# A decoder layer with four experts: the first tile of expert rows chosen from the first two batches, its choice spread over the last batch's scans

## The reference, cut to what matters

```python
x = layernorm(x + attention(x))          # 32 heads of 8, relative bias, softmax
x = layernorm(x + mamba(ctx_1024, z=x))  # conv, selective scan over 16 states, gated by silu(x)
# the experts, on all 1024 tokens:
probs = softmax(x @ Wr + br)             # 4 experts
top_w, top_idx = top_k(probs, 1)
y_e = (silu(x @ Wg[e]) * (x @ Wu[e])) @ Wd[e]   # 256 -> 1024 -> 256
out = y[top_idx] * top_w
x = layernorm(x + out)
```

## Time and profile before

| what | value |
|---|---|
| median of 3 runs | 473.2 us (471.0 to 474.16) |
| profiled execution, its own time | 473.93 us |
| its span in the profile | 472.2 us |
| PE busy | 420.8 us, 89% of the span |
| DVE, POOL, ACT busy | 312.3, 221.1, 211.2 us |
| chain that ended last | PE 66%, DVE 17%, POOL 6%, issue 5%, DMA 3%, ACT 2% |

### The profile page before, as it was taken

How to read it: one execution, slowest core, us unless ns; L and a number is a source line. 1 busy time by engine, 2 the same in 40 slices (tenths; PEclk the granted TensorE clock), 3 DMA queues, 4 the chain that set the end, 5 groups by cost and what they waited for, 6 DMA issues and landing times.

```text
span 472.2 us, 7846 instructions
## 1 busy us (share of the span) xinstructions
PE 420.8 (89%) x2560; PEld 212.2 (45%) x2561; DVE 312.3 (66%) x626; ACT 211.2 (45%) x412; POOL 221.1 (47%) x246
## 2 busy tenths in 40 slices
PE   4989588878998998989989899986999999999993
PEld 3444222333443443444434444354556666666652
DVE  3497778999987878878888786588214333334344
ACT  2456717564664557745577457612121111112220
POOL 2000615877986679967799578600551111111001
PEclk9998765798999999999999999999999999999997
DMA  9689940937365182756324430079120000000000
GB/s 237 91 279 108 301 144 12 146 119 115 89 138 110 68 134 70 134 180 199 137 78 169 159 112 0 1 287 361 55 55 11 12 4 9 11 11 11 11 1 9
DMA packets 39366, 49.36 MB, mean 105 GB/s; under 512 B 4664, under 2 KB 32673, under 8 KB 39334
## 3 DMA queue, kind: packets, MB, share of 16 engines
q1 hardware_dynamic: 36322, 46.65, 39.0%
q0 software_dynamic: 1056, 2.10, 1.5%
q10 hardware_dynamic: 1956, 0.21, 0.4%
HBM read 40.72 MB, written 8.91 MB: 105 GB/s over the span
## 4 chain that ended last, share of the span: by engine, by line
PE 66%; DVE 17%; POOL 6%; issue 5%; DMA 3%; ACT 2%; POOLq 0%; SPq 0%; DVEq 0%; ACTq 0%
PE ps L1181 16%; PE ps L1197 8%; PE ps L883 8%; PE ps L910 6%; PE ps L914 5%; PE ps L956 4%; PE ps L783 4%; DVE arena L1572 3%; DVE arena L1523 3%; DVE arena L1505 3%; PE ps L943 3%; PE ps L1189 2%; DMA arena<-arena 2%; POOL arena L655 2%; POOL arena L661 2%
## 5 line engine op out<-in xcount | busy, mean ns | idle before, releaser
L1372 ACT ACTIVATE arena<-ps 128x512 f32<-128x512 f32 x128 | 76.1, 595 | 84.9 <-PE ps L943 84.7
L1523 DVE TENSOR_REDUCE arena<-ps 128x2 f32<-128x512 f32 x128 | 86.6, 681 | 26.8 <-PE ps L914 22.7
L661 POOL TENSOR_TENSOR arena<-arena 128x512 f32<-128x512 f32 x60 | 76.8, 1279 | 36.2 <-DVE arena L1572 36.2
L655 POOL TENSOR_TENSOR arena<-arena 128x512 f32<-128x512 f32 x64 | 84.4, 1321 | 9.0 <-issue 8.8
L1181 PE MATMUL ps<-arena 128*128 x176 | 77.5, 593 | 0.7 <-ACT arena L1413 0.7
L1572 DVE TENSOR_TENSOR_SCAN arena<-ps,arena 128x512 f32<-128x512 f32 x60 | 72.8, 1214 | 0.5 <-DVE mv L1617 0.2
L883 PE MATMUL ps<-arena,identf 128*128 128x512 f32 x128 | 68.9, 625 | 0.0
L910 PE MATMUL ps<-arena 48*128 48x256 bf16 x256 | 52.7, 288 | 13.4 <-DVE arena L1523 10.0
L1331 ACT ACTIVATE ps<-arena 128x255 f32<-128x255 f32 x128 | 60.4, 473 | 1.9 <-DVEq L1726 1.9
L1839 DVE TENSOR_TENSOR arena<-arena,ps 128x1024 f32<-128x1024 f32 x11 | 13.4, 1222 | 59.9 <-ACT arena L1417 59.9
L731 POOL DMA_INDIRECT out<-rows_s,arena x11 | 10.8, 984 | 88.7 <-DVE rows_s L1868 80.5
(11 more groups left out here) (231 smaller groups left out, 524.7 us busy)
## 6 DMA issues: line engine op xcount, KB each, us to landing
arena<-bc_d SPq DMA_DIRECT2D x32, 512.0 KB, 4.4
arena<-in_L_ffn_Wg SPq DMA_DIRECT2D x8, 512.0 KB, 6.1
arena<-in_L_ffn_Wu SPq DMA_DIRECT2D x8, 512.0 KB, 5.9
arena<-in_L_ffn_Wd SPq DMA_DIRECT2D x4, 1024.0 KB, 11.7
arena<-kp_d SPq DMA_DIRECT2D x8, 384.0 KB, 7.9
arena<-qp_d SPq DMA_DIRECT2D x8, 384.0 KB, 10.8
qp_d<-arena SPq DMA_DIRECT2D x4, 384.0 KB, 8.5
kp_d<-arena SPq DMA_DIRECT2D x4, 384.0 KB, 8.4
```

The source lines that it names most:

```text
L655: g.tensor_tensor(dBu[m % 3], dtu[:, :, b * SEQ:(b + 1) * SEQ], over_k(bcr[c % BC_RING][:, m % 2, 0, :]), ALU.mult).then_inc(dbu_ready, 1)
L661: g.tensor_tensor(h, h, over_k(bcr[m // 2 % BC_RING][:, m % 2, 1, :]), ALU.mult).then_inc(hc_ready, 1)
L1372: A(prob[2 * (slot % 2) + kt][:, pr * HALF:(pr + 1) * HALF], ps[:, 2 + n % 2, :], ACT.Exp).then_inc(p_ready, 1)
L1523: v.tensor_reduce(negm[b % 2][:, qt, 2 * pair:2 * pair + 2], ps[:, bank, :].rearrange("p (h k) -> p h k", h=2), axis=AX.X, op=ALU.max).the ...
```

## The change

The 4 token tiles of batches 0 and 1 (EARLY) hold 512 tokens for 4 experts, so at least one expert has 128 of them. The changed kernel finds the first such expert (`estar`) and the first 128 of its tokens while the last batch is still being scanned, and makes of them tile 0. Four things follow.

- `early_step(n)` puts one small DVE operation at each step (qd, i) of the last batch from (2, 1) on, n = 4 qd + i - 9; n = 10 is empty, 21 operations in all. Operation 11 takes a PSUM bank from PE, which has computed the counts there (`count_early`, a turn more at (5, 0)). `early_ranks` (7 operations) and `early_marks` (4) stand behind the loop. POOL's `routing_constants` moves from scan 56 to scan 49 and gets 4 more small memsets.
- PE picks tile 0 (`pick_rows` over 4 tiles) behind the last attention outputs, ahead of the late logits, and runs gate_up(0) in four halves between the later steps of the routing, in place of most of the `keep_warm` there: one half ahead of the last router matmuls, two ahead of the counts, one behind them. ACT's `take_x(0)` moves ahead of `put_late(0)`; the wait for `wgu_in` moves with the first half.
- The tile that `first_rows` picks is now tile 1. DVE's `make_h(0)` stands between these marks and the index, `turn_h(0)` on PE between the picking and the index; one DVE operation sets tile 0's expert. POOL gathers rows for tiles 2, 0, 1 first.
- PE's loop over tiles begins at 2 and not at 1; ahead of it stand gate_up(1), down(0), turn_x(2), turn_h(1). The number of tiles stays 11.

```diff
+                        if b == BATCH - 1 and (qd, i) == (5, 0):
+                            count_early()
...
+            def gate_up_half(half, e):
+
+                w, fh = (wg_s, wu_s)[half // 2], half % 2
+                for k in range(KT):
+                    last = mm(ps[:, half, :], xcur[:, k, :], w[:, bass.ds((e * KT + k) * DFF + fh * HALF, HALF)],
+                              start=(k == 0), stop=(k == KT - 1))
+                return last
+
+            def pick_rows(tiles, marks, ready):
+
+                for t in range(tiles):
+                    pe.wait_ge(ready, t + 1)
+                    for k in range(KT):
+                        last = mm(ps[:, 7, k * P:(k + 1) * P], xres[:, t, k * P:(k + 1) * P], marks[t],
+                                  start=(t == 0 and k == 0), stop=(t == tiles - 1), skip_group_check=True)
+                last.then_inc(xt_pe, 1)
...
+            pe.wait_ge(y_out, BATCH)
+            pick_rows(EARLY, early_rows, early_ready)
...
+            pe.wait_ge(early_oh, 2)
+            first_expert = pe.value_load(estar_int[0:1, 0:1], min_val=0, max_val=EXPERTS - 1)
...
-            keep_warm(2, 5)
+            pe.wait_ge(wgu_in, 16 * 16)
+            pe.wait_ge(xcur_ready, 2)
+            gate_up_half(0, first_expert)
             route_late(BATCH - 1)
-            keep_warm(10, 7)
-
+            for half in (1, 2):
+                gate_up_half(half, first_expert)
 
             pe.wait_ge(oh_ready, 1)
             pe.wait_ge(consts, 4)
             oh_cols = ohb.rearrange("p e t -> p (e t)")
             mm(ps[:, 5, 0:EXPERTS * TT], ltri, oh_cols, start=True, stop=True)
             mm(ps[:, 6, 0:EXPERTS * TT], ones_b, oh_cols, start=True, stop=True).then_inc(count_pe, 1)
-            keep_warm(14, 4)
+            gate_up_half(3, first_expert).then_inc(gu_done, 1)
+            keep_warm(4, 4)
 
...
+            pick_rows(TT, first_rows, first_ready)
+            turn_h(0)
             pe.wait_ge(expert_ready, 1)
-            first_expert = expert_of(0)
+            second_expert = expert_of(1)
...
+            pe.wait_ge(xcur_ready, 3)
+            for half in range(4):
+                last = gate_up_half(half, second_expert)
+            last.then_inc(gu_done, 1)
             pe.wait_ge(wd_in, 16 * 4)
-            with pe.Fori(1, SLOTS - 1) as s:
+            down(0, expert_of(0))
+            turn_x(2)
+            turn_h(1)
+            with pe.Fori(2, SLOTS - 1) as s:
...
+            act.sem_inc(xcur_ready, 1)
+            act.sem_inc(gu_done, 1)
+            take_x(0)
             put_late(0)
...
                     scale_of(b - 2, mean2_ready, rstd2_ready)
                 if m == STATES * BATCH - 1:
                     scale_of(BATCH - 2, mean2_ready, rstd2_ready)
-                if m == 3 * STATES + 8:
+                if m == 3 * STATES + 1:
                     routing_constants()
```

(The last piece is POOL's place for the constants.) On DVE:

```diff
+                if n == 0:
+                    dve.wait_ge(taken, turns.count)
+                    link(v.tensor_reduce(lmax[:, two], lg[:, two, :], axis=AX.X, op=ALU.max))
+                elif n == 1:
...
+                    if n == 9:
+                        dve.wait_ge(logit_dve, 1)
+                        dve.sem_inc(early_oh, 1)
+                elif n == 11:
+                    bank = turn()
+                    link(v.tensor_copy(counts1.rearrange("p c n -> p (c n)"), ps[:, bank, 0:2 * EXPERTS * EARLY]))
+                    dve.sem_inc(taken, 1)
...
+                elif n == 21:
+                    v.tensor_copy(estar_int, estar).then_inc(early_oh, 1)
...
+            def early_ranks():
+
+                of_best = best.rearrange("p (e o) -> p e o", o=1).broadcast_to([P, EXPERTS, EARLY])
...
+            def early_marks():
+                for t in range(EARLY):
+                    v.tensor_scalar(early_rows[t], lanes, float(P + 1), lane1[:, t:t + 1], ALU.add,
+                                    ALU.is_equal).then_inc(early_ready, 1)
...
+                        if b == BATCH - 1 and qd >= 2:
+                            early_step(4 * qd + i - 9)
...
                             put_max(*eight_at(b, qd))
+            early_ranks()
+            early_marks()
...
-            link(v.tensor_tensor_scan(out=tile_incl, data0=ones32[:, 0:EXPERTS], data1=ntile, initial=0.0,
+            link(v.tensor_tensor_scan(out=tile_incl, data0=ones32[:, 0:EXPERTS], data1=ntile, initial=1.0,
...
             link(v.tensor_tensor(within, within, ohb, ALU.mult))
-            link(v.tensor_reduce(pos, within.rearrange("p e t -> p t e"), axis=AX.X, op=ALU.add))
+            link(v.tensor_reduce(pos, placed.rearrange("p e t -> p t e"), axis=AX.X, op=ALU.add))
             for t in range(TT):
-                v.tensor_scalar(first_rows[t], lanes, float(P), pos[:, t:t + 1], ALU.add, ALU.is_equal).then_inc(first_ready, 1)
+                v.tensor_scalar(first_rows[t], lanes, float(2 * P), pos[:, t:t + 1], ALU.add, ALU.is_equal).then_inc(first_ready, 1)
+            make_h(0)
...
+            link(v.tensor_tensor(e_of[:, 0:1], e_of[:, 0:1], estar, ALU.add))
             v.tensor_copy(e_int, e_of).then_inc(expert_ready, 1)
```

More of the change, by code:

```diff
@@ L216, in decoder_layer @@
         run = carve(TT)
-        within = carve(EXPERTS * TT, EXPERTS, TT)
+        placed = carve((EXPERTS + 1) * TT, EXPERTS + 1, TT)
+        within, of_early = placed[:, 0:EXPERTS, :], placed[:, EXPERTS, 0:EARLY]
+        incl1 = carve(EXPERTS * EARLY, EXPERTS, EARLY)
+        within1 = carve(EXPERTS * EARLY, EXPERTS, EARLY)
+        counts1 = carve(2 * EXPERTS * EARLY, 2, EXPERTS * EARLY)
+        resets1 = carve(EXPERTS * EARLY, EXPERTS, EARLY)
+        enough = carve(EXPERTS)
+        reached1 = carve(EXPERTS + 1)
+        best = carve(EXPERTS)
+        estar = carve(1)
+        estar_int = carve(1, dt=I32)
+        rank1 = carve(EARLY)
+        lane1 = carve(EARLY)
+        keep = carve(EARLY)
+        early_rows = [carve(P) for _ in range(EARLY)]
         incl = carve(EXPERTS * TT, EXPERTS, TT)
@@ L1199, in down @@
                 last.then_inc(y_done, 1)
-            pe.wait_ge(wgu_in, 16 * 16)
-            gate_up(0, first_expert)
-            turn_x(1)
-            keep_warm(8, 6)
-            turn_h(0)
+            pe.wait_ge(xcur_ready, 3)
+            for half in range(4):
+                last = gate_up_half(half, second_expert)
+            last.then_inc(gu_done, 1)
             pe.wait_ge(wd_in, 16 * 4)
-            with pe.Fori(1, SLOTS - 1) as s:
+            down(0, expert_of(0))
+            turn_x(2)
+            turn_h(1)
+            with pe.Fori(2, SLOTS - 1) as s:
                 gate_up(s, expert_of(s))
@@ L1709, in put_logits, with first_of_max @@
                                 ALU.add).then_inc(taken, 1)
+            def first_of_max(tiles):
+                link(v.tensor_copy(run[:, tiles], oh[:, tiles, 0]))
+                v.tensor_copy(ohb[:, 0, tiles], oh[:, tiles, 0]).then_inc(logit_dve, 1)
+                for e in range(1, EXPERTS):
+                    link(v.tensor_tensor(ohb[:, e, tiles], oh[:, tiles, e], run[:, tiles], ALU.is_gt))
+                    link(v.tensor_tensor(run[:, tiles], run[:, tiles], oh[:, tiles, e], ALU.max))
@@ L1777, in _ @@
             link(v.tensor_tensor(lg, lg, lmax3, ALU.subtract))
[L1778 to L1782 removed]
+            first_of_max(slice(EARLY, TT))
             dve.sem_inc(oh_ready, 1)
```

126 lines of the change are left out of this document (83 added, 43 removed).

## The result

The changed kernel takes 468.59 us (median of 20 runs, 465.85 to 471.48), the kernel before 472.54 us (20 runs, 469.82 to 474.63): ratio 0.9924, 95% interval 0.9907 to 0.9942. It is faster by 0.8%, some 3.6 to 4 us, where the forecast was 7.8. The profiled execution took 468.15 us, its span is 466.3.

The account below looks back on a forecast made before the run. It took the experts' stage, PE alone at 11.42 us a tile, as the bound. With 11.4 us saved and 3.6 paid, a gain of 7.8 put the profiled execution at 466.1, median 465.4; range 462.8 to 468.8.

Parts of the forecast that it names:

- DVE's steps: Last batch on DVE: 21 small operations at 0.2 us each, 4.2 us if all paid, 0 if all hidden.
- contention by instruction: Rival, chance 0.04: twelve steps beside POOL's chain each stop a product by 0.46 us, gate 5.5 us late: 470.9.
- POOL's constants: On POOL ahead of scan 51: memsets of about 3.0 us moved there cost 0.1 us, 3.0 if the scan waited.
- the bank's turn: Counts at (5, 0) in the last batch: PE's next turn of the PSUM bank 0.9 us later, part swallowed by idle time.
- ranks and marks: DVE behind the last batch's loop: 11 operations, 2.2 us, covered by 3.16 us of idle time, so they cost nothing.
- early picking: PE behind the last projection: 4 tiles picked in 1.9 us, of which 0.5 us come through.
- first half, weights: PE ahead of the last router matmuls: half of gate_up(0), 1.72 us, costs 0; weights landed by 319.5, just in time.
- halves two and three: Two halves of gate_up(0) on PE ahead of the counts: 322.8 to 326.2, delaying the counts by 0.4 us.
- the weights' rival: Rival, chance 0.04: up weights land near 331 us, PE waits at the first half, everything behind 10.7 us later: 476.3.
- nothing paid: Variant for the last batch: idle time swallows the turn and the steps fit, 1.0 us less: 464.3; 0.70 together with the forecast.
- A longer last batch: Rival, chance 0.20: on DVE, steps, bank's extra turn and constants delay each other, 5.0 us more: 470.4.
- the signs of being wrong: PE standing still at the first half, last-batch scans moved 3 us or more, or index after 337 through silu in make_h(0).

Follow-up runs that it names:

- the first run of the other form: Changed kernel, choice by three reduces, one comparison for three experts, counts read from PSUM, steps in their old places; first of two runs: 468.97 us.
- the choice in its better form: Changed kernel, choice by reduces, one comparison, counts read from PSUM, a running maximum, and steps moved to other places: 464.74 us.

## Why the prediction was wrong

**The step that failed** is the first sentence of "DVE's steps": 0.2 us each from start to start. The marks and the 0.17 of the earlier trace rows were measured behind the loop, where POOL is idle; the steps run behind scans, and a scan is what releases POOL's product. I had noted that collision and priced it by elements, "0.01 each". Measured: 6.1 us of excess on DVE, 2.57 us at the tail's copy where 0.4 stood, 4.9 in all where 1.0 stood. Some 3 of the 3.9 us too little are these waits; about 0.9 is left without a cause shown.

**The rows that misled me** are the earlier trace rows. I read a product of 1.73 us in place of 1.27 as a loss spread over 512 elements. Read the rows ahead of them too, DVE's and then POOL's, in the kernel before:

```profile
68.37 0.68 DVE L1505 SCALAR_TENSOR_TENSOR arena<-arena 128x512 f32<-128x512 f32 x1
```

```profile
75.84 3.73 POOL L655 TENSOR_TENSOR arena<-arena 128x512 f32<-128x512 f32 x3 [8.77 <-issue]
```

The same DVE operation takes 0.68 us where POOL is idle, and 1.25 at 78.87. So it had itself waited, for the product that ended at 75.84 + 3.73 = 79.57; it ended 0.55 us behind that, at 80.12. The next product ended at 79.52 + 1.73 = 81.25, which is 1.13 later, about a product's own length: it fits a product which was no slower but had waited for DVE. Whoever came second stood, on either side, and the trace of before had it. The rival "contention by instruction" had the right unit, the instruction, but the wrong side: in the last batch of the changed kernel POOL's products stayed at 1.26 to 1.28, and DVE stood.

The Trainium skill has this rule: "SBUF — State Buffer", "SBUF: two separate sides", says that the pair of ports which VectorE and GpSimd share is locked for a whole instruction by whichever starts first, while the other stands; its section "Who interferes with whom" counts in VectorE operations with two SBUF inputs or in a two-port mode, and leaves out the reduce. The runs agree where POOL starts first: 1.27 us for 128x4 elements, 0.65 with halved products, 0.15 for a reduce. Where VectorE starts first, the product of 1.73 us fits it.

The other steps, by the forecast and the runs:

| step | forecast us | measured |
|---|---|---|
| POOL's constants | 0.1 | 0.0: scan 51 starts 0.61 behind the start of DVE's reduce ahead of it, before (258.95) as after (258.12); add_mixed at 40.26 with the choice out, 40.24 before |
| the bank's turn | 0.9, part swallowed | a wait of 0.54 at 290.61; not run by itself |
| ranks and marks | 0, covered | 0: behind them DVE still waited 0.38 us for PE |
| early picking | 1.9 long, 0.5 paid | 1.95 at 314.90; 0.2 paid with the choice out (the last logits on DVE 63.18 behind scan 51, 63.00 before) |
| register load | 0, covered | 0: 0.486 at 318.2, beside the warm-ups |
| first half, weights | just in time | a wait of 0.19 at 323.57 |
| halves two and three | 0.4 | DVE waits 0.39 for the counts at 330.01; no wait with the choice out |
| make_h(0) | no wait for silu | none, at 333.84 |
| gate_up(1) to gate_up(2) | 11.7 | 350.92 - 339.33 = 11.6 by the chain |
| all but the choice | 8.8 gained | 9.87 |

Two sums of the prediction are off, neither with a share in the miss. The terms paid add up to 2.8, not 3.6: the tile that goes takes 10.6 us from gate_up(0) to gate_up(1), 334.44 to 345.07, as no down stands in it, and not 11.42. And the weights' rival is 465.4 + 10.7 = 476.1, not 476.3.

So the mechanism outside the choice was as forecast (a tile out of the loop, the period unchanged), and the rivals of the weights and of "nothing paid" are out. "A longer last batch" has the right place, and its interval (466.5 to 470.4) holds the measured time, but its reason, steps that add up unhidden, is not what the traces show. That 468.59 lies just inside the range of 462.8 to 468.8 is owed to the half of this rival that the range took in, and to the 1.0 us that all else came out better; it is luck, not the forecast. One of the signs of being wrong came true: the last scan starts 47.71 us behind scan 51, in place of 42.70, 5.0 later. The index came at 338.00, later than 337, but by the late batch and not by silu.

**What stays open.** By medians and by stretches the gains differ by up to 1.4 us (after: 3.95 and 4.99 us), and by some 3 us in the kernel with halved products and in the first run of the other form. I have one profiled execution of each kernel, and what varies early in the program, the same in all of them, I did not look into. The bank's turn is not priced by itself, nor is the 1.87 us that is left of the choice in its better form (89.02 - 87.15), where the forecast had 1.0.

## What to carry to other kernels

A tiny VectorE operation is not cheap by being tiny: if it reads two SBUF tensors, or copies or scales from SBUF to SBUF, beside GpSimd products it waited here for up to one whole product, with 3 to 16 elements. A reduce, or a sum with one input in PSUM, cost its own 0.13 to 0.2 us: change the form first and only then the place. And take a short operation's price from a row where the neighbours run as they will, comparing ends, not lengths.

## What the runs showed of the hardware

- An idle PE does not always lose its clock: it waited 2.54 us at 283.33 in the changed kernel, and the granted clock from 282 to 288 us was 1.00; with the choice left out a wait of 1.93 us at 298.94 was followed by 0.81, 0.50 and 0.84 in the next stretches of 2 us, and with all steps behind the loop one of 3.36 us by 0.79 and 0.56 in the stretches of 308 to 312 and 312 to 314 us. What tells these apart these rows don't show.
- An operation of 128x512 on DVE with both inputs in SBUF took 0.68 us with POOL idle and 1.25 beside a product of POOL, ending 0.55 behind it; the product behind it took 1.73 in place of 1.27.
- A product of 128x512 on POOL took 1.27 us, two of 128x256, the second awaiting the first, 1.53.
- bn_stats from SBUF, like a reduce, ran in 0.17 us beside a product.
